# Moving checks, the relations' parts and ten subtractions from VectorE to GpSimd in a two-network graph kernel

## What is computed

```python
deg_isqrt = max(segment_sum(1, dst), 1) ** -0.5
h = relu(layernorm(x))
x = x + L0(h, rel_embed, deg_isqrt, src, dst, edge_type)   # two layers, each:
#   msg = (rel_embed[type] + h[src]) @ W_r;  agg = segment_sum(msg, dst)
#   h = rrelu(agg * norm + where(in_degree == 0, h @ W_el, h @ W_sl))
h = relu(layernorm(x))
x = x + L1(h, src, dst, ...)   # attention over the edges with a softmax by segment
#   then @ Wo, residual, layer norm with gamma and beta
```

## Time and profile before

| | |
|---|---|
| median of three runs | 777.44 us |
| the profiled execution | 778.66 us, of which its span 776.9 us |
| TensorE matmul busy | 717.6 us (92%) |
| VectorE busy | 518.2 us (67%) |
| ScalarE busy | 431.4 us (56%) |
| GpSimd busy | 247.5 us (32%) |

### The profile page before, as it was taken

One profiled execution on the slowest core, in us unless ns is written; L12 is line 12 of the kernel. 1 busy time (PEld: TensorE's weight loads), 2 busy tenths in 40 slices (PEclk: granted clock), 3 DMA queues, 4 the chain that ended last, 5 costly groups with the idle time before them and its releaser, 6 DMA issues.

```text
span 776.9 us, 15463 instructions
## 1 busy us (share of the span) xinstructions
PE 717.6 (92%) x5799; PEld 534.0 (69%) x5799; DVE 518.2 (67%) x928; ACT 431.4 (56%) x1088; POOL 247.5 (32%) x274
## 2 busy tenths in 40 slices
PE   4676799999999999989999999799999999999996
PEld 3555688999899999889898998244444444444455
DVE  5999999998888877343234334245675757576576
ACT  1567566766666665642112222377676767767663
POOL 7230000000001222200000000366676757666665
PEclk7555599999999999999999999799999999999999
DMA  4101000133300000102221111110010100000010
GB/s 132 49 19 50 18 3 9 42 104 66 107 29 9 9 8 8 68 14 79 88 97 41 36 39 59 66 30 1 2 25 1 27 1 14 14 14 13 2 26 21
DMA packets 39763, 27.89 MB, mean 36 GB/s; under 512 B 5311, under 2 KB 38288, under 8 KB 39686
## 3 DMA queue, kind: packets, MB, share of 16 engines
q1 hardware_dynamic: 38514, 25.89, 11.4%
q10 hardware_dynamic: 1172, 0.98, 0.4%
HBM read 13.28 MB, written 10.80 MB: 31 GB/s over the span
## 4 chain that ended last, share of the span: by engine, by line
PE 75%; DVE 9%; issue 5%; ACT 5%; DMA 2%; POOL 2%; ACTq 0%; POOLq 0%; DVEq 0%; SPq 0%
PE sums L1542 17%; PE sums L1525 16%; PE sums L1038 12%; PE sums L1111 12%; PE sums L1077 8%; DVE work L863 3%; DVE work L857 3%; DMA x_after_messages<-work 2%; PE sums L1045 1%; PE sums L1139 1%; ACT counts L1313 1%; PE sums L1052 1%; PE sums L1118 1%; POOL counts L671 1%; POOL counts L699 1%
## 5 line engine op out<-in xcount | busy, mean ns | idle before, releaser
L1621 POOL TENSOR_TENSOR counts<-counts,work 125x500 f32<-125x500 f32 x150 | 164.8, 1099 | 100.3 <-DVE work L1691 95.0
L1077 PE MATMUL sums<-work 125*128 125x196 f16 (+15 forms) x1220 | 153.8, 253 | 21.1 <-DVE work L863 21.1
L1691 DVE SCALAR_TENSOR_TENSOR work<-sums,counts 125x500 f32<-125x500 f32 x150 | 101.6, 677 | 104.5 <-ACT sums L1645 99.0
L1542 PE MATMUL sums<-work 125*128 125x500 f32 (+1 forms) x350 | 159.7, 546 | 6.8 <-DVE work L1691 6.1
L1525 PE MATMUL sums<-work 128*125 128x500 f32 x300 | 152.2, 589 | 0.0
L1640 ACT ACTIVATE sums<-sums,steady 125x500 f32<-125x500 f32 (+1 forms) x157 | 102.0, 650 | 74.7 <-PE sums L1525 71.6
L1313 ACT CAST counts<-sums 128x364 f32 (+38 forms) x305 | 131.9, 473 | 2.2 <-issue 1.0
L857 DVE TENSOR_TENSOR work<-work,counts 125x3024 f16<-125x3024 f16 (+1 forms) x60 | 114.3, 1905 | 26.0 <-PE sums L1079 25.2
L1079 PE MATMUL sums<-work 125*128 125x10 f16 (+15 forms) x800 | 131.5, 194 | 0.0
L863 DVE TENSOR_TENSOR work<-work,counts 125x4200 f16<-125x4200 f16 (+15 forms) x120 | 125.5, 1086 | 0.0
L1038 PE MATMUL sums<-counts 125*128 125x250 f16 (+1 forms) x975 | 119.6, 266 | 3.7 <-ACT work L1243 3.5
(11 more groups left out here) (181 smaller groups left out, 694.6 us busy)
## 6 DMA issues: line engine op xcount, KB each, us to landing
first_columns<-counts SPq DMA_DIRECT2D x5, 610.4 KB
counts<-first_columns SPq DMA_DIRECT2D x5, 610.4 KB
counts<-counts SPq DMA_DIRECT2D x5, 468.8 KB
counts<-in_x SPq DMA_DIRECT2D x5, 312.5 KB
h_nodes<-counts SPq DMA_DIRECT2D x5, 312.5 KB
work<-in_x SPq DMA_DIRECT2D x12, 125.0 KB
x_after_messages<-work SPq DMA_DIRECT2D x12, 125.0 KB
h_attention<-work SPq DMA_DIRECT2D x12, 125.0 KB
```

The costliest lines, as they stand in the source:

```text
L1077: pe.matmul(win[:, 0:c, cols], lo[:, k * 2 * LO:k * 2 * LO + 128], m[:, k, h0 * w:(h0 + c) * w].rearrange("p (h d) -> p h d", d=w), start= ...
L1542: last = pe.matmul(ps_o[c % 2][:, 0:cols(u) // n], h3[:, source(c, j + i), :], pbuf[u % PB][:, i * NP:i * NP + cols(u) // n], start=j + i ...
L1621: pool.tensor_tensor(a, a, p, ALU.add).then_inc(acc_done, 1)
L1691: dve.scalar_tensor_tensor(pbuf[u % PB], ps_s[u % 4][0:NP, 0:WIDE], float(np.exp(-CLIP)), counts[0:NP, source(c, j), target(c) * WIDE:(tar ...
```

## The change

- The checks leave VectorE. GpSimd makes differences instead of comparisons: two of them (`steps_i`, 999 columns, and `far_i`, 40) after its tables and before it waits for the statistics; nine small linked instructions after the power -0.5. The table `least` with its twelve selects is moved behind the power too. ScalarE sums what lies above zero with its accumulator (`over_zero`): twice between its copies of the keys and group 0, twice at group 41. TensorE's sum over partitions moves from group 16 to group 44, and the flag from batch 6 to batch 13.
- The relations' parts (three casts and three subtractions of 256 columns, linked) move to GpSimd, behind the checks.
- All ten subtractions of the rests (640 columns) move to GpSimd, behind the relations, in the order of the groups in `ROUNDS`.
- The small tiles move to places where counts are not written so early.

```diff
+            pool.wait_ge(edges_in[0], 16)
+            pool.tensor_copy(final, dst_i[:, EDGES - 1:]).then_inc(outside_set, 1)
+            pool.tensor_tensor(steps_i[:, 1:], dst_i[:, :-1], dst_i[:, 1:], ALU.subtract).then_inc(outside_set, 1)
+            every = lambda v: v.rearrange("p (c e) -> p c e", e=MOST_STEP)[:, :, 0]
+            pool.wait_ge(dst_2_in, 16)
+            pool.tensor_tensor(far_i, every(dst_i[0:ROWS - 2, :]), every(dst_2), ALU.subtract).then_inc(outside_set, 1)
             pool.wait_ge(tables_done, 1)
             pool.wait_ge(stats_done, 1)
             pool.tensor_tensor(rstd, rstd, power.broadcast_to([NP, NB]), ALU.pow).then_inc(root_x, 1)
+            by_group(least, [(0, 0.0)] + [(READY[c], float(LB * NP * (c + 1))) for c in range(CHUNKS - 1)])
+            link(pool.memset(most[:, RT + 5:], 0.0))
+            pool.wait_ge(words_done, 1)
+            pool.wait_ge(outside_set, 5)
+            link(pool.tensor_copy(nx[:, 0:RT - 1], base[:, 1:]))
+            link(pool.tensor_copy(nx[:, RT - 1:], nxt_i))
+            link(pool.tensor_tensor(most[:, RT + 4:RT + 5], final, nx[:, RT - 1:], ALU.subtract))
+            link(pool.tensor_tensor(reached, nx, tb, ALU.subtract))
+            link(pool.tensor_tensor(by_tile(reached), by_tile(reached), over(w_c), ALU.subtract))
+            link(pool.tensor_tensor(most[:, 0:RT], tb, base, ALU.subtract))
+            link(pool.tensor_tensor(most[:, RT:RT + 2], by_tile(base)[:, :, 0], limit, ALU.subtract))
+            link(pool.tensor_tensor(most[:, RT + 2:RT + 4], least, by_tile(base)[:, :, 0], ALU.subtract))
+            pool.tensor_copy(most[0:1, RT + 5:], base[0:1, 0:1]).then_inc(outside_set, 1)
+            pool.wait_ge(outside_set, 6)
+            pool.wait_ge(rel_in, 16)
+            for s in range(3):
+                pool.tensor_copy(rel_parts[:, :, s, :], rel_f).then_inc(rel_step, 1)
+                pool.wait_ge(rel_step, 2 * s + 1)
+                pool.tensor_tensor(rel_f, rel_f, rel_parts[:, :, s, :], ALU.subtract).then_inc(rel_step, 1)
+                pool.wait_ge(rel_step, 2 * s + 2)
             pool.memset(half, -0.5).then_inc(pool_step, 1)
             steps[0] += 1
+            parts_t = parts1(0)
+            for g in sorted(ROUNDS[0] + ROUNDS[1]):
+                s = int(g in ROUNDS[1])
+                i = ROUNDS[s].index(g)
+                v = slice(5 * i, 5 * i + 5)
+                pool.wait_ge(rounded1[s], i + 1)
+                if s == 0:
+                    pool.wait_ge(h_out[i], 16)
+                    pool.tensor_tensor(xs[:, v, :], xs[:, v, :], parts_t[:, v, 0, :], ALU.subtract).then_inc(rest1[0], 1)
+                else:
+                    pool.tensor_tensor(parts_t[:, v, 2, :], xs[:, v, :], parts_t[:, v, 1, :], ALU.subtract).then_inc(rest1[1], 1)
...
-                if b == 1:
-                    checks()
                 if b == 2:
                     statistics()
-                if b == 11:
-                    relations()
...
-                if b == 6:
+                if b == 13:
                     dve.wait_ge(outside_sum, 1)
                     dve.tensor_scalar(T["flag"][:, :], psum[0:1, 7, 0:1], 0.0, None, ALU.is_gt).then_inc(flagged, 1)
-                for i in range(5):
-                    v = slice(5 * i, 5 * i + 5)
-                    if b == RESTS[0][i]:
...
+            def over_zero(k, out, v, least):
+                act.activation(out, v, ACT.Relu, bias=least, accum_out=outside[0:v.shape[0], k:k + 1]).then_inc(outside_ready, 1)
...
+            act.wait_ge(outside_set, 4)
+            over_zero(0, t_f[:, 1:], steps_i[:, 1:], 0.0)
+            act.wait_ge(outside_set, 5)
+            over_zero(1, hi[0:ROWS - 2, 0:EDGES // MOST_STEP], far_i, 1.0)
```

More of the change, by code:

```diff
@@ L257, in messages @@
     iota_f = place(14, 100, 128, NB * WM + WM % 2, I32)
-    junk = place(15, 100, ROWS, EDGES, F32)
+    steps_i = place(15, 100, ROWS, EDGES, I32)
     zeros = place(17, 100, 128, 512, F16)
     dst_2 = place(20, 100, ROWS - 2, EDGES, I32)
-    same = place(21, 100, ROWS - 2, EDGES // MOST_STEP, F32)
+    far_i = place(21, 100, ROWS - 2, EDGES // MOST_STEP, I32)
     small_at = 100
@@ L267, in tiny, with kept @@
         return place(16, small_at - 2 * cols, ROWS, cols, dt)
-    base, tb, nx, starts = (tiny(RT) for _ in range(4))
+    kept_at = 0
+    def kept(cols):
+        nonlocal kept_at
+        kept_at += cols
+        return small.rearrange("p k j -> p (k j)")[0:ROWS, kept_at - cols:kept_at]
+    base, tb, nx = (kept(RT) for _ in range(3))
+    limit, least, w_c, gb = (kept(2) for _ in range(4))
+    final, nxt_i, reached, most = kept(1), kept(1).bitcast(I32), kept(RT), kept(RT + 2 + 2 + 1 + 1)
+    starts = tiny(RT)
     group_i = tiny(RT, I32)
-    gb, after, room, limit, least, w_c = (tiny(2) for _ in range(6))
-    words, nxt_i = tiny(2, I32), tiny(1, I32)
-    bad = tiny(1 + 1 + 2 * RT + 2 + 2 + 1 + 1)
+    after, room = (tiny(2) for _ in range(2))
+    words = tiny(2, I32)
+    outside = T["outside"]
     by_tile = lambda v: v.rearrange("p (h t) -> p h t", h=2)
@@ L348, in messages @@
     SCALED = 16
+    CHECKED = 41
     ROUNDS = ((23, 29, 36, 43, 50), (33, 37, 45, 53, 57))
     scaled_after = {SCALED + j * 7 // 5: j for j in range(NB)}
-    RESTS = ((8, 9, 11, 13, 14), (10, 11, 13, 15, 16))
     R = {n: sem("r_" + n) for n in ("begin", "edges", "ramp", "prep", "hot", "used", "block_sum", "block_out", "again", "deg", "deg_step",
@@ L692, in _ @@
             pool.iota(iota_f, pattern=[[1, NB * WM + WM % 2]], base=0, channel_multiplier=0).then_inc(iota_done, 1)
-            by_group(least, [(0, 0.0)] + [(READY[c], float(LB * NP * (c + 1))) for c in range(CHUNKS - 1)])
             pool.memset(carry[:, 0, :], 0.0).then_inc(carry_ready, 1)
             pool.memset(ones_h, 1.0).then_inc(outside_set, 1)
-            pool.memset(T["outside"][:, :], 0.0).then_inc(outside_set, 1)
+            pool.memset(outside[:, :], 0.0).then_inc(outside_set, 1)
+            pool.wait_ge(edges_in[0], 16)
[4 more added lines that the diff above has]
+            pool.tensor_tensor(far_i, every(dst_i[0:ROWS - 2, :]), every(dst_2), ALU.subtract).then_inc(outside_set, 1)
             pool.wait_ge(tables_done, 1)
@@ L762, in _ @@
             dve.tensor_copy(iota_h, iota_f[0:NP, :])
[L764 to L785, removed]
             dve.wait_ge(next_in, 16)
@@ L804, in statistics @@
                 dve.tensor_scalar(rstd, mv[:, :, 1], EPS, None, ALU.add).then_inc(stats_done, 1)
[L806 to L812, removed]
             parts_t = parts1(0)
@@ L872, in _ @@
                 if b == 1:
-                    checks()
-                if b == 2:
                     statistics()
-                if b == 11:
-                    relations()
                 if b == 4:
@@ L1088, in _ @@
                     last.then_inc(summed, 1)
-                    if g == 16:
+                    if g == CHECKED + 3:
                         pe.wait_ge(later_keys, 12)
-                        pe.wait_ge(outside_ready, 1)
-                        pe.matmul(psum[0:1, 7, 0:1], T["outside"][:, :], one, start=True, stop=True).then_inc(outside_sum, 1)
+                        pe.wait_ge(outside_ready, 4)
+                        for k in range(4):
+                            last = pe.matmul(psum[0:1, 7, 0:1], outside[:, k:k + 1], one, start=k == 0, stop=k == 3)
+                        last.then_inc(outside_sum, 1)
                     if g == FIRST_SLOT:
@@ L1288, in _ @@
                 buf = psum[:, 2 * (g % 3):2 * (g % 3) + 2, :]
+                if g == 0:
+                    act.wait_ge(outside_ready, 2)
                 if g == KEY_GROUP:
@@ L1319, in _ @@
                     act.activation(xs[:, j, :], xs[:, j, :], ACT.Relu, bias=shift_x[:, j:j + 1], scale=rstd[:, j:j + 1]).then_inc(normed, 1)
+                if g == CHECKED:
+                    act.wait_ge(outside_set, 6)
+                    over_zero(2, reached, reached, 1.0)
+                    over_zero(3, most, most, 0.0)
                 for s in range(2):
@@ L1824, in program @@
              "work": sb("work", [128, WORK // 4], F32),
-             "ident_h": sb("ident_h", [128, 128], F16), "small": sb("small", [NP, 3, NB], F32), "outside": sb("outside", [NP, 1], F32),
+             "ident_h": sb("ident_h", [128, 128], F16), "small": sb("small", [NP, 3, NB], F32), "outside": sb("outside", [NP, 4], F32),
              "flag": sb("flag", [1, 1], I32), "steady": sb("steady", [128, 2], F32)}
```

## The result

| | before | after |
|---|---|---|
| median | 777.42 us (777.26 to 777.83, 4 runs) | 789.25 us (788.37 to 789.92, 4 runs) |
| ratio | | 1.0159, 95% interval 1.0142 to 1.0176 |
| profiled execution | 778.66 us, span 776.9 | 788.37 us, span 786.6 |

The change makes the kernel 11.8 us slower; 788.4 was forecast, with 780 to 793 as the range. That the number came out within 1 us is partly luck: two errors, of 4.8 and 6.4 us, nearly cancel.

What follows compares the result with a forecast made beforehand. VectorE bounds until about 98 us, then TensorE. Batch 17 late by 12.5 - 2.35 - 5.2 + 6.0 = 10.95 us: profiled 778.66 becomes 789.6, median 788.4 us; range 780 to 793, own range 785 to 791.5.

Steps and rivals of the forecast that it cites:

- The checks fill a wait: Before batch 2: the checks' 5.12 us filled a wait for TensorE, so batch 2 starts 0.9 us later, at 29.85.
- Statistics, power and batch 5 follow in the same pattern: After batch 2: the delay carries through unchanged, so batch 5 starts at 45.41 + 1.0 = 46.4 us.
- the 1.4 + 0.4 of the sum: Before batch 2: 1.4 us for ScalarE's two accumulating Relus, 0.4 us for `steps_i` delaying `words` and the key copies.
- Two reading GpSimd instructions per batch: Beside saturated VectorE: GpSimd's SBUF readers get in at comparison ends, two per batch; 28 queued ones need 14 batches.
- the 0.6 us taken: Batches 5 to 10: twelve GpSimd selects hold VectorE some 0.05 us each, 0.6 us together.
- The 2.3 us of the other reckoning: Batches 5 to 10: by the skill's shared-port rule, selects hold VectorE some 0.19 us each, 2.3 us together; end 790.1.
- The stop: After batch 10: VectorE idle from 67.2, first rest done at 75.95, batch 11 at 80.35, 12.5 us late.
- Subtractions hold VectorE: Each 1.36 us GpSimd subtraction costs saturated VectorE 1.2 us, more than the 0.74 saved; five hold it, 6.0 us.
- the rival in which GpSimd waits but doesn't hold: Stop as forecast, but VectorE loses nothing to the five late subtractions: 4.95 us late, 782.4 us; chance 0.10.
- The step that lets five run beside batches 11 to 16 for 6.0 us: Subtractions after groups 43 to 57 run beside batches 11 to 16 and cost VectorE 6.0 us.
- From there on nothing is shorter: After batch 17: TensorE leads, so the 10.95 us lateness stays to the end; profiled execution 778.66 becomes 789.6 us.
- four instructions through per batch: Rival of cancelling gains and losses: 24 done at the stop, rest 4 us shorter, end 781 to 782; chance 0.04.

Runs made afterwards that it cites:

- e10_flag: e1_early with VectorE's one-element instruction for the flag after batch 15 instead of 13; 778.33 us, ratio 1.0013 to the kernel before.
- e1_early: Changed kernel with checks, table least and relations ahead of GpSimd's wait for the statistics, only subtractions behind the power; 782.91 us, ratio 1.0073 to the kernel before.
- the kernels with the short queue: Kernels with checks and relations ahead of GpSimd's wait for the statistics, only subtractions left behind the power; e1_early, the changed kernel so reordered, took 782.91 us.
- e6_split: e1_early with the first rests of pieces 0 and 4 as five subtractions of 128 columns instead of one of 640; 784.09 us, ratio 1.0108.
- e3_both: Changed kernel with checks and relations ahead of GpSimd's wait for the statistics and the ten subtractions back on VectorE; 774.67 us, ratio 0.9960 to the kernel before.
- e8_transfers: e3_both with x loaded ahead of the second copy of the destinations and the relations' embedding ahead of x; 773.40 us, ratio 0.9959 to the kernel before.

## Why the prediction was right, and where it was not

- **The checks fill a wait.** Right in kind; wrong in place. Batch 5 was predicted at 46.4 and came at 44.40, because the statistics now fill the wait. The failed step is "Statistics, power and batch 5 follow in the same pattern": a misread diff, not a misread trace. The Relus and their accumulator outputs end 1.4 us after they begin, as predicted, and ScalarE's first copy of a carry comes at 28.37 us, 1.8 later than before, which is the 1.4 + 0.4 of the sum. `steps_i`, 2.63 us from 16.32, held one small instruction of VectorE on the way to `words` for 1.3 us (1.44 instead of 0.16); VectorE's wait after batch 1 absorbed it.
- **Two reading GpSimd instructions per batch.** Right: twelve selects in 19.35 us. As the power was done at 41.6 instead of 46.2 us, 15 instead of 12 were through when VectorE stopped. They held VectorE even less than the 0.6 us taken: batches 5 to 10 with the 0.19 us wait took 20.5 us, where 20.15 was reckoned without any hold. The 2.3 us of the other reckoning did not show.
- **The stop.** VectorE stopped at 64.9 (67.2 predicted), the first rest was there at 71.4 (75.95), batch 11 started at 75.57 (80.35). It was late by 7.7 us, not 12.5. Of the 4.8 us, 2.3 are the earlier start of the stop and 1.3 the memset and three more instructions that were through; the rest is relations of 3.5 instead of 4.0 us, a pitch of 0.28 instead of 0.33, and 4.1 instead of 4.4 us from the wait's end to batch 11.
- **Subtractions hold VectorE.** Right, 1.1 us each for 1.2 taken: four holds in the rows of 77.75, 80.35 and 87.29, not five. Which ones hold was wrong: only the three of groups 23, 29 and 33 ran in the stop; those of 36, 37, 43 and 45 held VectorE, 4.4 us together where 6.0 was predicted, and those of 50, 53 and 57 ended in the second stop. The same rows rule out the rival in which GpSimd waits but doesn't hold.
- **What I did not have.** The step that lets five run beside batches 11 to 16 for 6.0 us assumed that a waiting instruction gets in at the next end. One didn't, for 10.75 us, and VectorE stood 8.02 us. From batch 11 to 17 VectorE should have gained 1.55 us and lost 4.8. So the lateness at batch 17 was 12.6 us, 10.95 predicted: minus 4.8 and plus 6.4.
- **From there on nothing is shorter.** Right to 3 us. The batches keep their 12.5 us to the end of the counting (the last starts at 308.3 before and 320.8 after), and the attention starts 12.6 us late; the span is 9.7 us longer, the medians 11.8. In this pair of profiles the granted clock from the start of the attention on was low (1.2 GHz) for less time: 0.96 on average over 490 to 530 us, where it was 0.87 over 480 to 520 in the kernel before. How much of the difference that makes no run separates.
- **A sum in the rivals.** With four instructions through per batch, the twelve that are done early are nine small ones and three of the relations, by the prediction's own prices 9 x 0.33 + 3 x 0.67 = 5 us, not 4. The chance of 0.04 does not hang on it.

## What to carry to other kernels

In these runs GpSimd isn't a free engine beside a VectorE that runs two-operand instructions from SBUF: a subtraction that reads there waits for an end and then holds VectorE for most of its own time, so that, moved away, it costs VectorE 1.1 us where it cost 0.74. Move work to GpSimd into stretches in which VectorE reads one operand or waits (here the statistics, where 3.5 us of GpSimd's work cost VectorE 0.3 us), and count the queue in front of the one instruction that someone needs, not the busy time. A stop elsewhere in the pipeline also frees the engine that causes it: sum such a chain up to the stop, and then at the free speed.

## What the runs showed that I had not expected

- A GpSimd instruction that waits for SBUF is not sure of its turn. Most got in at the next end of a VectorE instruction; others stood 6 to 31 us while 4 to 26 VectorE instructions passed, whatever their length (640, 256, 128 or 2 columns, subtraction or cast), and got in at the first gap.
- Moving one 0.14 us VectorE instruction, a one-element read of PSUM, past the moment took this from 9.63 to 1.59 us (e10 against e1). That it brings the state about is shown for batch 14 of the kernels with the short queue, by one profile without it there (e10_flag) against one with it at each level of the clock (e1_early, e6_split). For the changed kernel, where the kept-out subtraction starts 2.2 us behind the flag, it is likely and not tested. How the instruction does it is open. So is what shut GpSimd out in batch 8, where no such instruction stands, and whether the flag has a part in the 17.00 us of e3_both, which begin 13.8 us after it.
- The fastest kernels are those that leave the ten subtractions on VectorE: e3_both and e8_transfers, 0.4% under the kernel before.
